# New slots for every piece beside the scan in a fused token, scan and FFN kernel

## The chip, the cores and the metric

The kernel runs on one core of one Trainium2 chip. The metric is the device time of the core in microseconds (us); lower is better. Five engines work side by side, each through its own list of instructions in order: TensorE (PE), VectorE (DVE), ScalarE (ACT), GpSimd (POOL) and SyncE (SP), which here only issues DMAs. They meet by semaphores.

## The reference

32 images of 224 x 224 and 32 texts of 77 tokens of 256 go in. Cut to what matters:

```python
# 1 tokens: 14 x 14 patches of 16 x 16 x 3, layer norm (768), matmul to 256, layer norm
p = patches(x); y = layernorm(layernorm(p, g1, b1) @ W + bias, g2, b2)
h = concat([y, txt], axis=1)                     # 196 + 77 = 273 positions
# 2 scan, on every second position of layernorm(h)
xs = rmsnorm(layernorm(h)[:, ::2]) * g_norm
x_proj, gate = split(xs @ w_in.T + b_in)
for t in positions:                              # state: 32 x 256 x 64
    s = tanh(s * A + x_proj[t][:, :, None] * Bm)
    y[t] = s @ c_sum + Dv * x_proj[t]
h = h + repeat((y * silu(gate)) @ w_out.T + b_out, 2)
# 3 FFN on layernorm(h), int weights / 127, hidden 768
h = h + (silu(z @ w_gate.T) * (z @ w_up.T)) @ w_down.T
```

The scan is the part that can't be done out of order: each position needs the state of the one before.

## The kernel before, in words

Positions are taken in 20 groups of 14 (one row of patches of all 32 images, or 14 text tokens; the last group has 7). A group has 7 scan steps, since every second position is scanned. The work of a group is spread over several iterations of a software pipeline. In iteration i, group i+1's raw pixels are read and normalised (`ahead`), group i is turned, embedded and projected (`pre`), group i-1 is scanned (`scan`), group i-2 goes from the scan's output through attention's output, residual, normalisation and FFN up to the hidden product (`post`), and group i-3 is multiplied by the down weights and stored (`down`).

One iteration has 56 slots: 7 steps of 8 chunks. In each slot the scan does one *grow* on DVE (line 827, U = h * A, into one of four PSUM banks), one *drive* on PE (line 1380, adds x * B to the bank) and one *squash* on ACT (line 1093, h = tanh(U)). A grow waits for the squash of four slots before, which frees its bank. All other work is cut into pieces, and the dictionary `PLANS` gives for each piece the slot behind whose scan instruction it stands on its engine. There is one plan for each kind of iteration: "zero" (i = -1) and "first" (i = 0), which have no scan, so that slots are only an order; "second" (i = 1); "image" (12 iterations, i = 2 to 13); "text" (6 iterations); "last" (i = 20, four steps of scan) and "tail" (no scan). Within a slot the pieces stand in the order of the calls in the body. The slots of different engines aren't bound to each other: an engine runs on until a semaphore stops it.

Pieces that the text speaks of: `turn` (PE) and `xT_copy` (ACT) transpose normalised pixels, `embed` (PE) multiplies them by W, `average` (PE) and raw_means, raw_deviation, raw_variance, raw_shift (DVE) make the pixels' statistics, `normalise` (ACT and GpSimd) applies them. `tok_stats`, `tok_shift`, `ln_stats`, `ln_shift` (DVE) with `token_rsqrt`, `ln_rsqrt`, `token_tiles` (GpSimd) normalise tokens. `turn_xa`, `xaT_copy`, `project`, `x_copy`, `x_low_part` make the scan's input, which SP writes to memory and loads back spread out as x_diag: early steps at the end of the same iteration, late steps in the next. `gate_silu` and `skip_term` make the gate.

The scan's output is read out once a step by `read_step` (line 1390: 8 matmuls of fp32 into the bank Y, 16 records in the trace). It needs the eight squashes of its step. Its place is fixed: in slot 3 of the following step, and the last step's readout in slot 3 of the next iteration. `y_copy` (ACT, line 1099) takes Y out; SP writes it to y_scr and loads it back as yT (lines 707, 713), GpSimd's `gating` (1267, 1272) adds the skip term and multiplies by the gate, `attend` (PE) multiplies by w_out, and `residual` (DVE, line 959) adds the tokens, which SP loads (`res`, line 750) behind the stores of the output (743). Then res_stats, res_variance, res_shift, fx_apply, turn_fx, fxT_copy, fx_low_part; then six blocks of FFN: ffn_gate and ffn_up (PE), ffn_silu (ACT), ffn_product (DVE), act_high_part (ACT), act_low_part (GpSimd). In the next iteration `shrink` (PE) multiplies by the down weights once all six low parts are there, and `finish` (DVE, line 995) adds the result to res.

SP's order is written out in `sync_body` and isn't changed: raw loads, gate_in, y_scr writes, yT loads, out stores, res load, late x_diag, tok store, scan writes, early x_diag, gate store. GpSimd has an order of its own, `POOL_ORDER`.

Of the kernel before, what the change touches and what calls it, by code (L numbers as in the profile page):

```python
# [34 lines left out]
READ_AT = 3  # L35
# [20 lines left out]
def span(first, end):  # L56
# [11 lines left out]
        shrink=(1, 2, 3, 5, 7, 7, 7, 7), turn=(8, 8, 9, 13, 13, 13, 13, 14), attend=(16, 16), average=(17, 21),  # L68
        embed=(17, 17, 17, 20, 21, 23, 23, 24, 25, 25, 28, 28), turn_fx=(30, 30), ffn_gate=(34, 38, 39, 42, 46, 50),
        ffn_up=(34, 38, 42, 44, 50, 52), turn_xa=(37,), project=(39, 39, 46, 48), finish=(8, 11), raw_patch=(10, 10,  # L70
        11, 11, 11, 12, 12, 12, 12, 14, 14, 14, 16, 16), raw_means=(17,), raw_deviation=(21,), raw_variance=(23,),
        res_stats=(20,), res_variance=(22,), res_shift=(27,), fx_low_part=(34, 34), tok_stats=(26, 32),
        tok_shift=(27, 34), ln_stats=(35,), ln_shift=(37,), raw_shift=(27,), x_low_part=(43,), ffn_product=(37, 41,
        43, 46, 53, 55), y_copy=(2,), xT_copy=(8, 8, 9, 12, 12, 12, 12, 15), fx_apply=(26, 27, 28, 28),
        fxT_copy=(30, 30), tok_normalise=(26, 34), ln_apply=(34,), xaT_copy=(36,), x_copy=(39,), gate_silu=(48,),
        ffn_silu=(33, 37, 39, 43, 46, 50), act_high_part=(37, 40, 40, 46, 50, 53), normalise=(38, 39, 49, 49, 51,
        52, 53), residual=(19,)),
    "text": dict(
        shrink=(5, 5, 7, 8, 12, 13, 16, 16), attend=(22, 25), turn_fx=(34, 34), ffn_gate=(35, 39, 41, 45, 49, 50),
        ffn_up=(37, 40, 44, 47, 49, 52), turn_xa=(27,), project=(30, 30, 32, 32), finish=(15, 20), res_stats=(30,),  # L80
        res_variance=(30,), res_shift=(31,), fx_low_part=(36, 36), ln_stats=(23,), ln_shift=(27,), x_low_part=(43,),
        ffn_product=(40, 44, 47, 50, 54, 55), y_copy=(2,), fx_apply=(31, 31, 31, 31), fxT_copy=(32, 32),
        ln_apply=(26,), xaT_copy=(27,), x_copy=(30,), gate_silu=(31,), ffn_silu=(35, 38, 43, 46, 46, 49),
        act_high_part=(44, 51, 51, 54, 55, 55), residual=(30,)),
    "last": dict(
        shrink=(5, 6, 7, 7, 9, 13, 13, 17), attend=(22, 25), turn_fx=(37, 37), ffn_gate=(40, 46, 50, 54, 55, 55),
        ffn_up=(45, 46, 50, 54, 55, 55), finish=(15, 19), res_stats=(30,), res_variance=(32,), res_shift=(32,),
        fx_low_part=(36, 43), ffn_product=(50, 50, 50, 51, 55, 55), y_copy=(2,), fx_apply=(32, 32, 34, 39),
        fxT_copy=(39, 43), ffn_silu=(44, 47, 47, 53, 55, 55), act_high_part=(48, 49, 54, 55, 55, 55),
        residual=(30,), y_next=(55,)),  # L90
    "first": dict(
        turn=(1, 1, 1, 1, 1, 1, 7, 9), embed=(1, 4, 4, 10, 10, 12, 13, 16, 19, 23, 31, 34), weight_turn=(1, 1, 1,
        1), weight_copy=(1, 8, 16, 55), xT_copy=(0, 0, 0, 0), first_copy=(0, 1, 4, 13), tok_stats=(18, 45),
        tok_centre=(20, 35), tok_affine=(28, 36), tok_shift=(46,), tok_normalise=(16,), ln_stats=(40,),
# [92 lines left out]
def build(nc, x, txt, W, tok_bias, ln1_g, ln1_b, ln2_g, ln2_b, w_in, b_in, A, Bm, Cm, Dv, w_out, b_out,  # L187
# [8 lines left out]
    with ctx:  # L196
# [1546 lines left out]
```

## Time and profile before

| | us |
|---|---|
| median of the runs shown (3) | 1350.34 |
| lowest and highest | 1347.21, 1351.81 |
| profiled execution: span | 1347.8 |
| PE busy | 1203.9 (89%) |
| DVE busy | 1066.3 (79%) |
| ACT busy | 982.1 (73%) |
| POOL busy | 423.5 (31%) |

The span is the time from the first to the last instruction of one execution; the profile reports no time around it. An engine's busy time is the union of its instructions' times, from start to end; instructions that follow each other overlap at their ends, so a piece's spacing is shorter than its duration. A scan iteration is counted from its first grow to the next one's.

### The profile page before, as it was taken

To read this page: it belongs to the slowest core of one execution; us is meant where nothing else is said; L and a number is where in the kernel's file an instruction comes from. 1 tells how busy PE (TensorE), PEld (TensorE's weight loads), DVE (VectorE), ACT (ScalarE), POOL (GpSimd) and SP (SyncE) were. 2 spreads that over 40 slices of the span, in tenths; PEclk is the share of its full clock that TensorE was granted. 3 is DMA by queue.
4 is the path that set the end of the run, shared out by engine and by line. 5 is a ranking of instruction groups with operands and counts; after the bars stand their busy time and mean duration, and the time that the engine had idled before them with its cause. 6 is when DMAs were issued, how large, how long until landed. Compare 5 with 4: busy or idle time off the path is not lost.

```text
span 1347.8 us, 26044 instructions
## 1 busy us (share of the span) xinstructions
PE 1203.9 (89%) x7217; PEld 642.2 (48%) x7217; DVE 1066.3 (79%) x2423; ACT 982.1 (73%) x1944; POOL 423.5 (31%) x435
## 2 busy tenths in 40 slices
PE   6678898999999999999999999999999899998977
PEld 4434445454545464646464646464444444444435
DVE  4697888887878887888888878777888888887843
ACT  2357596969696969696969696968778788787752
POOL 6413152525252525252525252514121221321220
PEclk9779899999999999999999999999999999999989
DMA  7411414141414141414141414212322322322210
GB/s 173 130 28 36 102 49 103 49 102 49 101 49 101 49 101 49 101 49 101 49 101 49 101 49 101 62 47 63 82 72 66 104 56 79 93 65 61 63 43 27
DMA packets 154814, 99.60 MB, mean 74 GB/s; under 512 B 129072, under 2 KB 143536, under 8 KB 153424
## 3 DMA queue, kind: packets, MB, share of 16 engines
q1 hardware_dynamic: 151120, 97.58, 28.4%
q10 hardware_dynamic: 3648, 1.46, 0.5%
q8 instruction: 23, 0.38, 0.1%
q14 instruction: 23, 0.19, 0.0%
HBM read 58.39 MB, written 40.60 MB: 73 GB/s over the span
## 4 chain that ended last, share of the span: by engine, by line
PE 31%; issue 26%; POOL 18%; DVE 8%; ACT 7%; DMA 7%; SPq 2%; POOLq 1%; ACTq 0%; DVEq 0%
PE Y L1390 8%; PE U L1380 6%; POOL xT_act L1309 4%; DVE U L827 4%; DMA y_scr<-y_fx 4%; PE P L1560 3%; PE P L1561 3%; POOL rawn L1288 3%; PE P L1576 2%; ACT h L1093 2%; POOL raw_s L1256 2%; PE P L1577 2%; DMA yT<-y_scr 2%; POOL tok L1301 2%; POOL tok L1304 2%
## 5 line engine op out<-in xcount | busy, mean ns | idle before, releaser
L827 DVE TENSOR_TENSOR U<-h,a_col 128x512 f32<-128x512 f32 x1096 | 708.9, 690 | 145.6 <-ACT h L1093 138.9
L1093 ACT ACTIVATE h<-U 128x512 f32<-128x512 f32 x1096 | 609.2, 608 | 200.4 <-PE U L1380 198.5
L1380 PE MATMUL U<-x_diag,b_st 128*128 128x512 f16 x1096 | 363.1, 386 | 51.4 <-DVE U L827 49.8
L1390 PE MATMUL Y<-h,read_st 128*32 128x512 f32 x2192 | 268.7, 608 | 0.7 <-ACT h L1093 0.7
L1380 PEld LDWEIGHTS U<-x_diag,b_st 128*128 128x128 f16 x1096 | 104.1, 99 | 250.6 <-DVE U L827 198.4
L1309 POOL TENSOR_TENSOR xT_act<-act,xT_act 128x448 f16<-128x448 f32 x114 | 117.4, 1038 | 242.5 <-ACT xT_act L1202 242.5
L1456 PE MATMUL P<-tok_w,xT_act 128*112 128x256 f32 x648 | 158.7, 385 | 0.8 <-ACT xT_act L1117 0.8
L1456 PEld LDWEIGHTS P<-tok_w,xT_act 128*112 128x112 f32 x648 | 116.9, 181 | 31.5 <-ACT xT_act L1117 1.1
L1390 PEld LDWEIGHTS Y<-h,read_st 128*32 128x32 f32 x2192 | 57.8, 110 | 133.7 <-issue 117.0
L1576 PE MATMUL P<-down_w,xT_act 128*112 128x256 bf16 (+1 forms) x480 | 114.8, 277 | 5.9 <-POOL xT_act L1309 4.2
L1577 PE MATMUL P<-down_w,xT_act 128*112 128x256 bf16 (+1 forms) x480 | 113.7, 275 | 0.0
L1267 POOL TENSOR_TENSOR yT<-yT,gate_in 128x448 f32<-128x448 f32 x20 | 22.7, 1136 | 244.9 <-DMA yT<-y_scr 244.9
L1560 PE MATMUL P<-fx_split,gate_w 128*128 128x448 f16 x228 | 81.0, 355 | 12.0 <-DVE fx_split L990 10.6
L984 DVE SCALAR_TENSOR_TENSOR act<-fsg,P 128x448 f32<-128x448 f32 (+1 forms) x118 | 72.1, 611 | 21.2 <-PE P L1561 18.1
L1117 ACT ACTIVATE xT_act<-P 128x384 f32<-128x384 f32 x108 | 80.4, 795 | 8.4 <-PE P L1439 7.0
L1560 PE MATMUL P<-fx_split,up_w 128*128 128x448 f16 (+1 forms) x236 | 83.0, 353 | 0.7 <-DVE act L984 0.7
L1561 PE MATMUL P<-fx_split,up_w 128*128 128x448 f16 (+1 forms) x236 | 82.9, 352 | 0.0
L1197 ACT ACTIVATE fsg<-P 128x448 f32<-128x448 f32 x114 | 63.6, 558 | 24.4 <-PE P L1561 22.9
L1561 PE MATMUL P<-fx_split,gate_w 128*128 128x448 f16 x228 | 80.8, 354 | 0.0
L1256 POOL TENSOR_TENSOR res_s<-res_s,half_th 112x4 f32<-112x4 f32 x20 | 20.6, 1028 | 186.2 <-DVE res_s L973 186.2
L834 DVE BATCH_NORM_STATS2 raw_st<-raw 96x6 f32<-96x256 f32 x196 | 70.1, 409 | 10.0 <-DMA raw<-in_x 9.7
L1491 PE MATMUL P<-xaT,in_w 128*128 128x224 f32 x320 | 74.3, 370 | 1.7 <-ACT xf L1165 1.0
(165 smaller groups left out, 1469.1 us busy)
## 6 DMA issues: line engine op xcount, KB each, us to landing
raw<-in_x SPq DMA_DIRECT2D x42, 448.0 KB, 6.1
gate_scr<-gate_o SPq DMA_DIRECT2D x20, 448.0 KB, 2.5
gate_in<-gate_scr SPq DMA_DIRECT2D x20, 448.0 KB, 7.6
tok_scr<-tok SPq DMA_DIRECT2D x19, 448.0 KB, 3.1
res<-tok_scr SPq DMA_DIRECT2D x19, 448.0 KB, 3.7
out<-res SPq DMA_DIRECT2D x76, 112.0 KB, 2.3
x_diag<-scan_scr SPq DMA_DIRECT2D x312, 16.0 KB
x_diag<-scan_scr SPq DMA_DIRECT2D x304, 12.0 KB
```

The lines of the kernel that those rows point to most:

```text
L827: dve.tensor_tensor(U[bank_of(slot)][:, :].rearrange("p (l b) -> p l b", b=B), h[:, (slot - CHUNKS) % RING, :].rearrange("p (l b) -> p l b ...
L1093: sc.activation(h[:, slot % RING, :], U[bank_of(slot)][:, :], ACT.Tanh, scale=1.0 / U_SCALE).then_inc(squashed, 1)
L1117: sc.activation(xT[:, hf * CH:hf * CH + CH, par, :].rearrange("p c (b t) -> p t c b", t=STEPS)[:, t0:t0 + nt], P[turn_bank(n)][:, 0:nt * R ...
L1309: gp.tensor_tensor(act_lo[:, k, :], act[:, k, :], act_hi[:, k, :], ALU.subtract).then_inc(act_lo_done, 1)
L1380: pe.matmul(U[bank_of(slot)][:, :], b_st[:, c, :], x_diag[:, c, :, t * B:t * B + B], start=False, stop=True, skip_group_check=True).then_i ...
L1390: mm = pe.matmul(Y[c4 * 32:c4 * 32 + 32, :], read_st[:, t, half, :], h[:, (t * CHUNKS + half * RG + c4) % RING, :], start=(t == 0 and half ...
L1456: mm = pe.matmul(tok_bank(k // 2, g)[0:PT, (k % 2) * D:(k % 2) * D + D], xT[:, f, k // 2, (k % 2) * PT:(k % 2) * PT + PT], tok_w[:, f, :], ...
L1491: mm = pe.matmul(P[1][:, k * TOK:k * TOK + TOK], in_w[:, j, e0:e0 + 128], xaT[:, j, :], start=(j == 0), stop=(j == DB - 1))
L1560: pe.matmul(bank, half, fx_hi[:, j, 0:n], start=(j == 0), stop=False)
L1561: mm = pe.matmul(bank, half, fx_lo[:, j, 0:n], start=False, stop=(j == DB - 1))
L1576: pe.matmul(bank, act_hi[:, f, k * m:k * m + m], half, start=(f == 0), stop=False)
L1577: mm = pe.matmul(bank, act_lo[:, f, k * m:k * m + m], half, start=False, stop=(f == HB - 1))
```

## The change

Every list of slots in `PLANS` is new, and so is GpSimd's order. `read_step` becomes a piece with its own list, `read`: entry 0 is the readout of the last step of the iteration before, entry k that of step k-1. Two waits are added: raw_shift waits, in image iterations, until all eight turns of its group are done, and the FFN's first block waits for its inputs in the up half as well as in the gate half.

```diff
-READ_AT = 3
     "image": dict(
-        shrink=(1, 2, 3, 5, 7, 7, 7, 7), turn=(8, 8, 9, 13, 13, 13, 13, 14), attend=(16, 16), average=(17, 21),
-        embed=(17, 17, 17, 20, 21, 23, 23, 24, 25, 25, 28, 28), turn_fx=(30, 30), ffn_gate=(34, 38, 39, 42, 46, 50),
-        ffn_up=(34, 38, 42, 44, 50, 52), turn_xa=(37,), project=(39, 39, 46, 48), finish=(8, 11), ...
-        ... y_copy=(2,), xT_copy=(8, 8, 9, 12, 12, 12, 12, 15), fx_apply=(26, 27, 28, 28), ...
-        ... normalise=(38, 39, 49, 49, 51, 52, 53), residual=(19,)),
+        read=(0, 12, 18, 29, 33, 42, 51), shrink=(2, 2, 4, 5, 6, 6, 8, 8), turn=(8, 9, 10, 10, 11, 12, 13, 16),
+        attend=(16, 16), average=(18, 20), embed=(18, 19, 19, 20, 21, 22, 24, 24, 26, 27, 28, 28), turn_fx=(31,
+        32), ffn_gate=(35, 36, 39, 40, 47, 53), ffn_up=(35, 39, 42, 46, 51, 53), turn_xa=(38,), project=(40, 41,
+        47, 48), finish=(8, 11), ... y_copy=(0,),
+        xT_copy=(8, 8, 8, 10, 10, 12, 12, 17), fx_apply=(22, 24, 25, 29), ...
+        ... normalise=(28, 28, 28, 29, 42, 47, 49), residual=(19,)),
     "text": dict(
-        shrink=(5, 5, 7, 8, 12, 13, 16, 16), attend=(22, 25), turn_fx=(34, 34), ffn_gate=(35, 39, 41, 45, 49, 50),
-        ffn_up=(37, 40, 44, 47, 49, 52), ... finish=(15, 20), ... y_copy=(2,), ... residual=(30,)),
+        read=(0, 13, 21, 29, 36, 41, 53), shrink=(3, 4, 6, 8, 10, 15, 19, 20), attend=(23, 24), turn_fx=(39,
+        39), ffn_gate=(43, 45, 46, 48, 50, 51), ffn_up=(44, 45, 46, 48, 50, 51), ...
+        finish=(13, 22), ... y_copy=(0,), ... residual=(32,)),
     "last": ...
-        ... y_copy=(2,), ... residual=(30,), y_next=(55,)),
+        read=(1, 11, 19, 28), ... y_copy=(1,), ... residual=(40,), y_next=(40,)),
     "first": ...
-        ... weight_copy=(1, 8, 16, 55), ... raw_patch=(20, 20, 24, 24, ...), tok_stats=(18, 45), project=(44, 46, 46, 46),
-        clear_banks=(55,), clear_stage=(52,), ...
+        ... weight_copy=(7, 11, 17, 33), ... raw_patch=(11, 11, 16, 16, ...), tok_stats=(15, 42), project=(25, 39, 42, 50),
+        clear_banks=(43,), clear_stage=(11,), ...
     "second": ...
-        ffn_turn=(41, 43, 44, 47, 48, 51, 55, 55, 55, 55, 55), ... ffn_cast=(1, 2, 3, 7, 8), ffn_max=(5, 9, 23, 26, 31, 35),
+        read=(4, 8, 21, 27, 36, 44, 50), ffn_turn=(31, 36, 39, 40, 41, 45, 48, 49, 51, 53, 55), ...
+        ffn_cast=(0, 0, 0, 0, 0), ffn_max=(2, 4, 4, 5, 6, 21), ...
     # "tail", "zero" and POOL_ORDER: the same pieces in other places; clear_rest comes first in "first",
     # ln_rsqrt before token_rsqrt(1) in "image"
...
             def raw_shift():
                 dve.wait_ge(raw_rstd, r + 1)
+                if pre and image:
+                    dve.wait_ge(turned_ps, (g + 1) * 8)
...
             def ffn(k, which):
-                if k == 0 and which == 0:
+                if k == 0:
                     pe.wait_ge(fxT_done, (q + 1) * 4)
                     pe.wait_ge(fx_lo_done, (q + 1) * 2)
...
                     drive(slot)
-                    if slot % CHUNKS == READ_AT and slot >= CHUNKS:
-                        read_step(slot // CHUNKS - 1, s, steps)
-                    elif slot == READ_AT and due(s):
-                        read_step(STEPS - 1, s - 1, STEPS)
+                    for k in parts_at(plan, "read", slot):
+                        if k:
+                            read_step(k - 1, s, steps)
+                        elif due(s):
+                            read_step(STEPS - 1, s - 1, STEPS)
```

## Rows read from the trace of the kernel before

**Rows 1.** The page: busy time of an engine, and the chain that ended last.
```profile
PE 1203.9 (89%) x7217; PEld 642.2 (48%) x7217; DVE 1066.3 (79%) x2423; ACT 982.1 (73%) x1944; POOL 423.5 (31%) x435
...
PE 31%; issue 26%; POOL 18%; DVE 8%; ACT 7%; DMA 7%; SPq 2%; POOLq 1%; ACTq 0%; DVEq 0%
```
**Rows 2.** Windows: stretch, length, busy PE, PEld, DVE, ACT, POOL, clock, DMA share, GB/s.
```profile
0.00:62.60 62.60, 39.81 (x176) 26.66 (x177) 34.21 (x125) 16.75 (x30) 35.80 (x30) 0.89 0.56 143
62.60:135.20 72.60, 57.50 (x294) 28.61 (x292) 59.97 (x142) 46.01 (x88) 15.23 (x18) 0.88 0.20 48
...
672.80:740.20 67.40, 62.14 (x382) 34.46 (x381) 55.49 (x135) 52.44 (x105) 24.64 (x26) 1.00 0.30 75
1047.90:1100.90 53.00, 48.93 (x302) 23.35 (x301) 45.44 (x86) 42.84 (x86) 11.81 (x13) 1.00 0.29 80
```
**Rows 3.** Groups by line of the image iteration from 672.8: busy, mean ns, idle before.
```profile
L827 DVE TENSOR_TENSOR U<-h,a_col 128x512 f32<-128x512 f32 x56 | 36.5, 689 | 7.6 <-ACT h L1093 7.5
L1093 ACT ACTIVATE h<-U 128x512 f32<-128x512 f32 x57 | 32.2, 611 | 10.8 <-PE U L1380 10.8
...
L1456 PE MATMUL P<-tok_w,xT_act 128*112 128x256 f32 x48 | 11.5, 379 | 0.0
```
**Rows 4.** Waits of the same iteration: total, times, longest.
```profile
POOL yT L1267 <- DMA yT<-y_scr: 14.3, 1, 14.3
...
DVE U L827 <- ACT h L1093: 7.5, 12, 2.2
```
**Rows 5.** Timeline of PE in that iteration: start, length, instruction, idle before.
```profile
671.84 0.35 PE L1561 MATMUL P<-fx_split,up_w 128*128 128x448 f16 x1
...
674.82 0.32 PE L1576 MATMUL P<-down_w,xT_act 128*112 128x256 bf16 x1 [0.32 <-POOL xT_act L1309]
...
676.75 1.92 PE L1390 MATMUL Y<-h,read_st 128*32 128x512 f32 x16
678.60 0.32 PE L1576 MATMUL P<-down_w,xT_act 128*112 128x256 bf16 x1
...
694.37 0.38 PE L1380 MATMUL U<-x_diag,b_st 128*128 128x512 f16 x1
...
739.30 0.35 PE L1561 MATMUL P<-fx_split,up_w 128*128 128x448 f16 x1
```
**Rows 6.** Chain of waits in that iteration: start, length, what.
```profile
678.82 0.61 ACT y_fx L1099
...
681.03 4.60 DMA y_scr<-y_fx
...
686.35 2.52 DMA yT<-y_scr
```
**Rows 7.** Timelines of SP (DMA issues) and DVE in that iteration.
```profile
674.46 1.36 SPq L371 DMA_DIRECT2D raw<-in_x  x3
...
692.52 0.35 SPq L750 DMA_DIRECT2D res<-tok_scr  x1
...
696.48 1.23 DVE L959 SCALAR_TENSOR_TENSOR res<-P,res 112x1024 f32<-112x1024 f32 x1 [0.88 <-DMA res<-tok_scr]
```
**Rows 8.** Timeline of DVE in the text iteration from 1047.9.
```profile
1071.95 1.23 DVE L959 SCALAR_TENSOR_TENSOR res<-P,res 112x1024 f32<-112x1024 f32 x1
```
**Rows 9.** Timeline of the start: staging area cleared, x_lo, first drive.
```profile
52.52 2.30 DVE L457 MEMSET x_diag<- 128x2688 int32 x1 [0.74 <-issue]
...
54.74 0.56 DVE L949 SCALAR_TENSOR_TENSOR x_lo<-xf,x_hi 128x448 f16<-128x448 f32 x1
...
64.11 0.38 PE L1380 MATMUL U<-x_diag,b_st 128*128 128x512 f16 x1
```
**Rows 10.** Lines of FFN casts and maxima: duration ns min/median/max, first and last start.
```profile
L552 DVE CAST act<-act x2: 675/814/954, 63.8 to 65.5; 128x1536 f32<-128x1536 int32 x1, 128x1024 f32<-128x1024 int32 x1
...
L557 DVE TENSOR_REDUCE large<-act x2: 1214/1483/1752, 68.7 to 76.2; 128x1 f32<-128x1536 f32 x1, 128x1 f32<-128x1024 f32 x1
```
**Rows 11.** Timeline of GpSimd in the last iteration with FFN.
```profile
1315.51 1.13 POOL L1267 TENSOR_TENSOR yT<-yT,gate_in 128x448 f32<-128x448 f32 x1 [2.21 <-DMA yT<-y_scr]
```

More of the change, by code:

```diff
@@ L73 @@
[L73 to L77, printed above, removed]
-    "text": dict(
-        shrink=(5, 5, 7, 8, 12, 13, 16, 16), attend=(22, 25), turn_fx=(34, 34), ffn_gate=(35, 39, 41, 45, 49, 50),
[L80 to L84, printed above, removed]
@@ L85 @@
-    "last": dict(
[L86 to L90, printed above, removed]
-    "first": dict(
-        turn=(1, 1, 1, 1, 1, 1, 7, 9), embed=(1, 4, 4, 10, 10, 12, 13, 16, 19, 23, 31, 34), weight_turn=(1, 1, 1,
-        1), weight_copy=(1, 8, 16, 55), xT_copy=(0, 0, 0, 0), first_copy=(0, 1, 4, 13), tok_stats=(18, 45),
-        tok_centre=(20, 35), tok_affine=(28, 36), tok_shift=(46,), tok_normalise=(16,), ln_stats=(40,),
-        ln_shift=(44,), ln_apply=(3,), ln_apply_first=(47,), turn_xa=(42,), xaT_copy=(23,), project=(44, 46, 46,
-        46), x_copy=(25,), x_low_part=(54,), gate_silu=(55,), raw_patch=(20, 20, 24, 24, 26, 34, 34, 34, 36, 36, 38,
-        42, 44, 46), raw_means=(48,), average=(37, 43), raw_deviation=(50,), raw_variance=(51,), raw_shift=(51,),
-        normalise=(33, 36, 39, 39, 39, 43, 49), clear_banks=(55,), sum_c=(36,), read_scale=(55,), b_split=(5, 9, 9,
-        14, 18, 39), c_pair=(3,), clear_stage=(52,), diag_half=(51,), keep_busy=(52, 54, 55)),
@@ new lines @@
+    "last": dict(
+        read=(1, 11, 19, 28), shrink=(0, 3, 5, 7, 8, 15, 15, 16), attend=(22, 26), turn_fx=(34, 37),
+        ffn_gate=(38, 43, 49, 51, 52, 54), ffn_up=(41, 45, 49, 51, 53, 54), finish=(15, 19), res_stats=(41,),
+        res_variance=(43,), res_shift=(43,), fx_low_part=(44, 44), ffn_product=(45, 50, 50, 53, 53, 55),
+        y_copy=(1,), fx_apply=(32, 32, 33, 36), fxT_copy=(36, 37), ffn_silu=(37, 38, 44, 45, 49, 55),
+        act_high_part=(38, 44, 47, 54, 55, 55), residual=(40,), y_next=(40,)),
@@ new lines @@
+    "tail": dict(
+        shrink=(3, 4, 6, 9, 11, 18, 19, 21), attend=(11, 16), turn_fx=(24, 24), ffn_gate=(28, 32, 40, 46, 49,
+        55), ffn_up=(34, 39, 48, 51, 54, 55), finish=(0, 5), res_stats=(0,), res_variance=(0,), res_shift=(7,),
+        fx_low_part=(22, 28), ffn_product=(28, 29, 32, 47, 50, 52), fx_apply=(0, 6, 12, 13), fxT_copy=(29, 41),
+        ffn_silu=(42, 42, 47, 47, 53, 55), act_high_part=(43, 51, 51, 55, 55, 55), residual=(0,),
+        act_low_tail=(39, 44, 50, 52, 53, 55), keep_busy=(2, 20, 21, 26)),
@@ L119 @@
+        average=(8, 9), bias_part=(14, 22, 31, 35, 49, 54), normalise=(3, 13, 28, 30, 31), bias_add=(45,),
         keep_busy=(0, 0, 4)),
```

86 lines of the change are left out of this document (50 added, 36 removed).

## The prediction, made before the change was run

> **What bounds the kernel now.** I read the page first, then the stages by windows, then one steady image iteration by lines, waits, timeline and chain, then the start. The page has TensorE busy for 89% of the span, but the chain that ends last is 31% PE, 26% issue, 18% POOL, 8% DVE [rows 1]: no engine is the bound alone; the time is set by how four in-order queues are laid against each other. By windows a steady image iteration takes 67.4 us, with PE busy 62.1, DVE 55.5 and ACT 52.4; a text iteration 53.0 with 48.9, 45.4 and 42.8; the second iteration 72.6 with 57.5 and 60.0 [rows 2]. PE's busy time has the tails of its pipelined matmuls in it. Worked out by spacing instead (start to start where pieces follow each other), an image iteration has 56 drives of 0.22, seven readouts of 1.85 (676.75 to 678.60), 8 shrink pieces near 0.7, 12 embed pieces of 0.9 (the row gives at most 11.5/12) and some 17 us of turns, attend, FFN and projection: about 58 us. So some 9 us of 67.4 are PE waiting, which is the most that an order could give back [rows 2, 3, 5]. The waits between grow and squash are spread out: DVE waits 7.5 us for ACT in 12 pieces, and the longest single wait is GpSimd's, 14.3 us for yT to land [rows 4].
>
> **The image iteration, 12 of them, piece by piece.** The number of instructions is the same; only places change, plus two waits. I walked the new lists against the old ones in three stretches, each engine's pieces in order with the spacings above, and 0.1 us for each hand-over.
>
> *Head.* The last up piece is followed by three drives and then nothing until the first shrink piece at 674.82, 2.8 us later, because the shrink needs product, high part and GpSimd's low part of the last FFN block; five drives fill 1.1 of it, so PE loses 1.7 [rows 5]. The new list puts the previous step's last readout (1.85) at slot 0, in that hole. It can't start before squash 55, which I place 1.6 us after the last up piece: 1.1 us of waiting is left in place of 1.7, and the readout no longer stands between the shrink pieces. I put squashes 0 and 1 around y_copy: ACT waits for the readout at slot 0 instead of slot 2, 2 us in both. So the shrinks (slots 2 to 8) end at 1.7 + 1.85 for the readout + 8 x 0.69 + 8 drives of 0.22 = 10.8 us after the last up piece; before it was 11.5. From there to attend's end PE has a readout of 1.85, eight drives (1.8), eight turns (2.3) and attend (2.0), 8.0 us. Before it took 10.8, as turns waited for finish(1) and for xT copies; with the copies grouped (ACT slots 8, 10, 12) and the readout between the turns I leave 1.2 of waiting. Attend's end goes from 22.3 us (694.37) to 20.0 [rows 5].
>
> *The readout's own chain.* y_copy at 678.82 starts a chain of transfers: 4.60 us of y_scr, 2.52 of yT, then GpSimd's gating [rows 5, 6]. SP issues in order, so the out stores and the load of res stand behind it: res is issued at 692.52, and residual (696.48) still waited 0.88 us for it [rows 7]. The new y_copy comes 3.1 us earlier after the last up piece. Gating then ends before attend wants it, and the next lock on res is finish(1), whose store must have landed: finish(1) is 0.4 to 0.9 us earlier, and SP's queue 3. Residual's end goes from 25.6 us to between 22.7 (SP alone) and 24.1 (one wait of 1.2 at average kept). I take 24.1, being the nearer to the row.
>
> One rule speaks against this. Raw's three transfers are issued at 674.46 and gate_in's behind them, ahead of y_scr, and y_scr took 4.60 us to land [rows 6, 7]. The Trainium skill, "DMA: Bandwidth & Descriptors", section "Two DMAs through the same engine are not ordered", has descriptors of one queue start in order: an earlier y_scr would then only wait longer behind raw. By that rule the head start is lost unless raw moves too; it does (ACT's last normalise goes from slot 53 to 49), and I expect the head start to survive. Without it the sum would be rival 1's, worked out below.
>
> *From residual to the last up piece.* Before: from residual's end (696.48 + 1.14 of spacing = 697.62) to the end of the last up piece (739.30 + 0.19 = 739.49) it is 41.9 us; both ends by spacing, as the piece before ends at 672.03 [rows 5, 7]. New: PE does one readout before residual and two embed pieces more behind it, equal work. fx_apply(0) at slot 22 makes ACT wait for res_shift (DVE slot 25) with squashes 23 to 25 behind it, about 1.5 us, which PE's embed pieces cover; readout 4 at slot 33 and 5 at 42 wait 0.3 us for the squash; up 3 waits 0.8 us for product 2. With the same work as before my walk gives 41.6, so I claim almost nothing here. Together 24.1 + 41.6 = 65.7 against 67.4: -1.7 us each, -20 us for 12. Bounds: no gain, if the head start is absorbed at average; and -2.8.
>
> **Text, 6 iterations of 53.** FFN moves from slots 35 to 52 into 43 to 51, y_copy from 2 to 0, turn_fx to 39. Residual stood 24 us into the iteration (1071.95) [rows 8]; finish(1) at slot 22 puts it at about 28, and the 22.6 us behind it have to hold what took 27. I get 51.7 us: -1.2 each, rounded to -6 in all because this stretch has no slack left on PE; bounds +1 and -2 each.
>
> **Start.** The first drive is at 64.11 us [rows 9]. Ahead of it stand the clearing of the staging area by DVE (2.30 us from 52.52, just before x_lo at 54.74), weight_copy 3 and clear_banks behind ACT's DMA issues. The new list clears at slot 11, projects at 25 and 39 and has weight_copy 3 at 33. The price: DVE's raw_patch 0 to 3 now stand before tok_stats(0), and raw lands only near 34 us (estimated from the start's transfers), 1.8 us later than tok_stats ran. Net, x_hi and x_lo come 3 us earlier, the early x_diag lands near 60.3 and the first drive at 60.4: -3.7. Bounds 0 and -6.
>
> **Second iteration.** Casts of the FFN weights (median 0.81 for act) and the first maximum (1.75) sat on DVE in slots 1 to 8, in the path of grows [rows 10]. At slot 0 they, with bias_split 0 to 2, run while DVE would wait for the first drive; about 6 us of DVE's 60.0 [rows 2] leave the loop. ffn_turn, five of eleven at slot 55 before, starts at 31. Against it: readout 1 at slot 8 waits about 1 us for squash 7, and average(0) waits for 14 patches. I take -5.3; bounds +2 and -8.
>
> **Last and tail.** y_next moves ahead of most silus, so gating is bound by act_low 5 instead of yT, which it waited 2.21 us for [rows 11]: -2, bounds 0 and -3. GpSimd's new order costs nothing where it waits anyway [rows 4]; its act_low 5, the piece that PE waits for, stays last.
>
> **The two new waits.** turned_ps before raw_shift was met 10 slots before. The FFN wait on a second piece repeats one met a piece earlier. No wait here has an own row; 0 to 0.05 us for each of about 50, below 2.5 us. I take 0.
>
> **Sum.** -20 - 6 - 3.7 - 5.3 - 2 = -37. The profiled execution spans 1347.8 us with nothing reported around it, 2.5 below the median 1350.3 of the runs shown: 1347.8 - 37 = 1310.8, plus 2.5 is 1313.3.
>
> **Rivals.**
> 1. *The head start is absorbed.* y_scr still lands behind raw and gate_in, residual stays at 25.6 us. For: 4.60 us of landing beside raw. Against: residual's own wait of 0.88 us. Image gains 0.4 each: -5 - 6 - 3.7 - 5.3 - 2 = -22, 1328.
> 2. *Readouts block PE; slower.* A readout directly behind its step (slots 0, 33, 42 of image; 0, 29 and 41 of text) holds drive, squash and grow behind it, where the old place, three slots on, was free. It needs squash done, and ACT runs up to 2 us behind PE. Where that wait isn't covered, 0.9 us for each of three in 18 iterations is +49; with the forecast's -37 that is +12, so 1362. It decides from 37/54, about 0.7 us a readout; my walk has 0.3 for two of the three. For it: grows already wait for ACT in 12 places [rows 4]. Against: at slot 0 PE has nothing else to do.
> 3. *No change.* The loops refill as PE's own work binds behind residual (image 0, text +1), and only start and second count, partly: -3, 1347.
> 4. *Both locks open:* image -2.8, rest as above but start -6: 1297.
>
> **Chances.** Forecast 0.44, rival 1 0.20, rival 2 0.14, rival 3 0.10, rival 4 0.12. 0.3%, about 4 us, is what a measurement of this kernel can tell from no change. Faster 0.77, same 0.09, slower 0.14. The range 1293 to 1353 leaves out rival 2 and the far end of rival 4; the forecast's own range is 1303 to 1323.
>
> **What would show it.** Right: image iterations of 65 to 66 us; y_copy 5 us or less after the last up piece, residual 24 us after it; first drive near 60; second iteration under 68; PE's idle time at the first shrink under 1 us. Wrong: waits of PE for ACT h L1093 before Y over 1 us each; DVE waiting for res at an unchanged place; an image iteration at 67 or more; text over 53.

## The result, and the profile after

The kernel after takes 1288.61 us (median of 4 runs, 1286.47 to 1290.56), the kernel before 1351.07 beside it: a ratio of 0.9547, 95% interval 0.9528 to 0.9565, or 62.5 us less. The forecast was 1313.3, 37 less, with 1293 as the low end of its range: the sign was right, the size was short by 25 us, and the time lies 4 us below the range. The profiled execution took 1288.4 us and spans 1286.7.

The page of the kernel after, the lines that answer to [rows 1]:

```profile
PE 1193.1 (93%) x7217; PEld 643.8 (50%) x7217; DVE 1078.1 (84%) x2423; ACT 982.7 (76%) x1944; POOL 434.3 (34%) x435
...
PE 46%; DVE 16%; issue 14%; ACT 11%; DMA 5%; POOL 3%; SPq 2%; DVEq 1%; ACTq 0%; POOLq 0%
```

The work is the same (7217 matmuls, 2423 and 1944 instructions). What went is waiting: the chain was 31% PE and 18% POOL, it is now 46% PE and 3% POOL, so the order of the queues is closer to being bound by TensorE's own work. ACT's busy time didn't move; DVE's rose by 12 us, and that is a cost found below (x_lo).

Windows of the kernel after, with the columns of [rows 2]: the start, the second iteration, a steady image iteration and a steady text iteration. They are cut 0.4 us ahead of the first grows, which start at 54.97, 123.16, 640.56 and 997.85; the lengths are the same.

```profile
0.00:54.60 54.60, 37.00 (x155) 26.32 (x156) 32.71 (x124) 12.91 (x22) 29.31 (x21) 0.84 0.59 151
54.60:122.80 68.20, 58.58 (x316) 29.57 (x314) 63.72 (x141) 48.24 (x95) 25.08 (x27) 0.90 0.25 61
...
640.20:704.40 64.20, 61.66 (x383) 34.59 (x381) 56.35 (x135) 53.00 (x105) 25.31 (x26) 1.00 0.32 79
997.50:1049.10 51.60, 48.98 (x309) 23.24 (x305) 45.40 (x85) 42.08 (x87) 11.79 (x13) 1.00 0.30 80
```

PE's busy time in the image iteration is the same within 0.5 us (62.1 before); 67.4 us have become 64.2. Stretch by stretch, each from the first grow to the next iteration's first grow, beside what the prediction gave it:

| stretch | before | after | difference | forecast |
|---|---|---|---|---|
| start and second iteration | 135.2 | 123.2 | -12.0 | -9.0 |
| image, 12 iterations | 805.5 | 773.0 | -32.5 | -20 |
| text, 6 iterations | 322.4 | 309.1 | -13.3 | -6 |
| last and tail | 84.7 | 81.3 | -3.3 | -2 |
| sum | 1347.8 | 1286.7 | -61.1 | -37 |

Every term came out larger, and the image term has half of the whole miss. The walk through one image iteration can be read off the timelines of the kernel after, first DVE and SP (start, length, instruction, idle before):

```profile
644.53 1.87 SPq L709 DMA_DIRECT2D y_scr<-y_fx  x4
651.10 1.27 SPq L715 DMA_DIRECT2D yT<-y_scr  x2
652.77 3.23 SPq L745 DMA_DIRECT2D out<-res  x4
657.92 0.35 SPq L752 DMA_DIRECT2D res<-tok_scr  x1
...
661.71 1.22 DVE L963 SCALAR_TENSOR_TENSOR res<-P,res 112x1024 f32<-112x1024 f32 x1 [0.30 <-DMA res<-tok_scr]
```

and PE:

```profile
639.63 0.35 PE L1565 MATMUL P<-fx_split,up_w 128*128 128x448 f16 x1
639.82 0.59 PE L1384 MATMUL U<-x_diag,b_st 128*128 128x512 f16 x2
641.31 0.39 PE L1384 MATMUL U<-x_diag,b_st 128*128 128x512 f16 x1 [0.89 <-DVE U L829]
641.63 1.92 PE L1394 MATMUL Y<-h,read_st 128*32 128x512 f32 x16
...
660.16 0.59 PE L1384 MATMUL U<-x_diag,b_st 128*128 128x512 f16 x2
...
703.82 0.35 PE L1565 MATMUL P<-fx_split,up_w 128*128 128x448 f16 x1
704.01 0.38 PE L1384 MATMUL U<-x_diag,b_st 128*128 128x512 f16 x1
```

The last up piece ends at 639.82 by spacing. The readout stands in the hole behind it, and attend ends at 660.16, 20.3 us later (forecast 20.0, before 22.3). Residual waits 0.30 us for the load of res and ends at 661.71 + 1.14 = 662.85, that is 23.0 us, where the prediction had 24.1 and its lower bound 22.7. From there to the next last up piece (704.01) it is 41.2, forecast 41.6. The waits of that iteration, with the columns of [rows 4]:

```profile
POOL yT L1271 <- DMA yT<-y_scr: 11.6, 1, 11.6
...
ACT h L1097 <- PE U L1384: 8.1, 12, 1.8
...
DVE U L829 <- ACT h L1097: 4.1, 7, 1.2
```

DVE waited 7.5 us for ACT before, now 4.1; ACT waited 10.8 for PE, now 8.1 [rows 3, 4]. The engines of the scan wait less for each other.

### The profile page after: what moved, and what is told of

Same layout as the page of the kernel before. It is cut to its first block, busy times and chain, and to the rows that moved or that the text cites. A ratio compares the mean times of both kernels' runs of the same rounds, so it can differ in the third digit from the quotient of the medians.

```text
span 1286.7 us, 26087 instructions
## 1 busy us (share of the span) xinstructions
PE 1193.1 (93%) x7217; PEld 643.8 (50%) x7217; DVE 1078.1 (84%) x2423; ACT 982.7 (76%) x1944; POOL 434.3 (34%) x435
## 4 chain that ended last, share of the span: by engine, by line
PE 46%; DVE 16%; issue 14%; ACT 11%; DMA 5%; POOL 3%; SPq 2%; DVEq 1%; ACTq 0%; POOLq 0%
PE Y L1394 11%; PE U L1384 9%; DVE U L829 7%; PE P L1460 7%; ACT h L1097 5%; PE P L1564 5%; PE P L1565 4%; DMA raw<-in_x 3%; PE P L1580 2%; PE P L1581 2%; PE P L1443 2%; PE P L1495 2%; DMA y_scr<-y_fx 1%; PE P L1515 1%; ACT fsg L1201 1%
## 5 line engine op out<-in xcount | busy, mean ns | idle before, releaser
L1384 PE MATMUL U<-x_diag,b_st 128*128 128x512 f16 x1096 | 368.7, 383 | 42.6 <-DVE U L829 40.1
L1384 PEld LDWEIGHTS U<-x_diag,b_st 128*128 128x128 f16 x1096 | 101.3, 98 | 210.9 <-DVE U L829 153.5
L1460 PEld LDWEIGHTS P<-tok_w,xT_act 128*112 128x112 f32 x648 | 113.1, 177 | 41.4 <-ACT xT_act L1121 10.1
L1564 PE MATMUL P<-fx_split,gate_w 128*128 128x448 f16 x228 | 81.3, 356 | 3.0 <-DVE fx_split L994 1.9
L836 DVE BATCH_NORM_STATS2 raw_st<-raw 96x6 f32<-96x256 f32 x196 | 71.8, 410 | 9.9 <-DMA raw<-in_x 9.7
L1495 PE MATMUL P<-xaT,in_w 128*128 128x224 f32 x320 | 77.5, 369 | 1.3 <-ACT xf L1169 0.8
L1201 ACT ACTIVATE fsg<-P 128x448 f32<-128x448 f32 x114 | 63.4, 556 | 14.5 <-PE P L1565 13.2
```

What stands on the lines that cost most here:

```text
L1384: pe.matmul(U[bank_of(slot)][:, :], b_st[:, c, :], x_diag[:, c, :, t * B:t * B + B], start=False, stop=True, skip_group_check=True).then_i ...
L1460: mm = pe.matmul(tok_bank(k // 2, g)[0:PT, (k % 2) * D:(k % 2) * D + D], xT[:, f, k // 2, (k % 2) * PT:(k % 2) * PT + PT], tok_w[:, f, :], ...
L1495: mm = pe.matmul(P[1][:, k * TOK:k * TOK + TOK], in_w[:, j, e0:e0 + 128], xaT[:, j, :], start=(j == 0), stop=(j == DB - 1))
L1564: pe.matmul(bank, half, fx_hi[:, j, 0:n], start=(j == 0), stop=False)
```

## Experiments

All runs are beside runs of the kernel before on the same chip (1349.3 to 1349.7 us). Each kernel is the kernel after with one edit unless it is said otherwise. A result is given as its median, the ratio to the kernel before with its 95% interval, and how much more it is than the kernel after (1288.61, runs from 1286.47 to 1290.56, interval 0.9528 to 0.9565). Of u_end, d_res, u_cast and n_text the interval overlaps that of the kernel after: their differences of 0.2 to 3.4 us rest on the stretches of the traces more than on the times. The length of an iteration is that of most of them in the run's trace, from first grow to first grow.

### Which part brought how much

**u_image**: the image plan and GpSimd's image order as before, with readouts at their old places.

```diff
 PLANS["image"], POOL_ORDER["image"] = those of the kernel before
+read=(3, 11, 19, 27, 35, 43, 51), y_copy=(2,)
```

> The changed kernel with the plan and GpSimd's order of the image iterations as before (readouts at slots 3, 11, ..., 51); all else changed. Theory A, each kind of iteration gained by itself, as the two traces' stretches say (image 32.5 us of 61.5): 1288.6 + 32 = 1321 us, image iterations back at 67. Rival B, the gain of a stretch hangs on its neighbours' new plans (a head that is filled because the iteration before ends otherwise): clearly off 1321, under 1310 or over 1332. By the forecast on record (20 us for images) it would be 1309.

1323.27 us, ratio 0.9799 (0.9776 to 0.9822): 34.7 more than the kernel after, as theory A has it, and its steady image iteration takes 67.0 us. Its twelve take 805.4 us, where the kernel before has 805.5: the two added waits, which stand in this kernel, cost nothing there. **u_text** does the same to text:

> The changed kernel with the plan of the text iterations as before; all else changed. Theory A: text's share in the traces is 13.3 us, of which the four steady iterations hold 5.3 and the first and the last 8.0: 1302 us. Rival B: the first text iteration's 4.3 us were the image plan's doing, so only about 9 come back: 1298 us. By the forecast (6 us): 1295.

1306.48, 0.9682 (0.9653 to 0.971): 17.9 more, beyond theory A's 13. The four steady iterations are back at 52.9, the first one gives back 2.8 us, the sixth 3.6, and the first step of the last iteration, whose plan is not touched, 4.3. **u_start** does it to the plans zero, first and second:

> The changed kernel with the plans zero, first and second as before; all else changed. Theory A: 1288.6 + 12.4 = 1301 us, first drive at 64.1 us, second iteration 72.6 us. By the forecast (9 us): 1297.6. Rival: the second iteration's end loses what it ran ahead anyway at the first image iteration, and less than 6 us come back: under 1295.

1304.11, 0.9666 (0.9644 to 0.9689): 15.5 more, with four runs from 1299.15 to 1306.46; the profiled one is the lowest, and its stretch to the end of the second iteration is 11.5 longer. **u_end** does it to last and tail:

> The changed kernel with the plans last and tail as before; all else changed. Theory A: 1288.6 + 3.3 = 1292 us, gating of the last group bound by yT again (a wait near 2.2 us). Rival: last and tail are bound by the same chain either way, and the 3.3 us came from the text plan's earlier end: under 1290.

1291.76, 0.957 (0.955 to 0.9591): 3.2 more, as theory A has it, though gating waits 1.1 us for yT in place of the 2.2 named there. The four add up to 71.3 against 62.5: between the kinds of iteration the change is nearly additive. Within one kind it is not, as the next runs show.

### The head, and the rule on the queue

**u_head** takes back only the head of image and text: `read[0]` to slot 3, `y_copy` to 2.

> The changed kernel, only the last step's readout back from slot 0 to slot 3 and y_copy from 0 to 2 in image and text. Theory A, the head start of the readout's chain is what frees the image iteration: residual moves back by 2 to 3 us, image iterations by 2 or more, text by 0 to 1: 1288.6 + 24 to 36, about 1318 us. Rival B, the hole is filled but the rest of the new list makes the gain: +0.6 an iteration, about 1300 us. Rival C, the new head costs ACT as much as it gives: within 4 us of 1288.6.

1303.22, 0.9665 (0.9649 to 0.9681): 14.6 more, of which the image iterations have 10.3, at 65.38 each. Nearest to rival B. Residual, 667.42 in the timeline of DVE below, ends 23.8 us after the last up piece (644.74) in place of 23.0, and no longer waits for res:

```profile
667.42 1.18 DVE L968 SCALAR_TENSOR_TENSOR res<-P,res 112x1024 f32<-112x1024 f32 x1
```

So the readout's move is worth 1.2 of the 3 us in this place. **b_head** makes the same move alone in the kernel before: `read[0]` and `y_copy` to slot 0.

> The kernel before (all its plans, old GpSimd order), with one thing new: the last step's readout at slot 0 and y_copy at 0 in image and text. Theory A, the chain behind y_copy bounds the image iteration: 2 us for each of 12, 0.5 for text: about 1351 - 27 = 1324 us. Rival B, the old list can't use an earlier residual, and only the hole is filled: 0.6 us in 18 iterations, 1340 us. Rival C, nothing or slower, as ACT's wait at y_copy now stands before squash 1: 1350 or more.

1364.88, 1.0117 (1.01 to 1.0134): slower than before by 15.5 us, which is rival C; 10.8 of it is in the image iterations and 1.6 in text, and 3.6 stands ahead of the first image iteration, where the plans are those of before. It is the kernel after's code with the plans of before, so the two added waits are in it. Windows of two image iterations of this kernel, with identical instructions:

```profile
477.20:545.60 68.40, 63.37 (x383) 34.85 (x381) 55.64 (x135) 52.72 (x105) 24.69 (x26) 0.98 0.30 74
682.60:749.80 67.20, 61.89 (x383) 34.56 (x381) 55.62 (x135) 52.67 (x105) 24.64 (x26) 1.00 0.30 75
```

The second takes what an iteration took before. The first has its readout 0 at a lower clock, in PE's timeline:

```profile
478.20 0.39 PE L1403 MATMUL U<-x_diag,b_st 128*128 128x512 f16 x1 [0.68 <-DVE U L848]
479.84 3.32 PE L1413 MATMUL Y<-h,read_st 128*32 128x512 f32 x16 [1.25 <-ACT h L1116]
```

16 records took 3.32 us where they take 1.92; the granted clock from 479.7 to 483.0 was 0.58, most of it at the lower level of 1.2 GHz. Ahead of it PE had waited 0.68 us for DVE and 1.25 for ACT, since in the old order ACT is later: squash 0 starts 2.2 us after the first grow, in the kernel after 1.2. Of the ten image iterations from 273.33 on, all with the wait of 1.2 us for ACT, eight have a readout 0 of 2.8 to 3.6 us and two one of 1.92. So the head move gains nothing by itself, and loses 1.2 us where the clock falls; text loses 0.5 an iteration at a granted clock of 1.00. It pays only with ACT ahead, as it is in the new order; which of ACT's pieces does that no run separates. That is the mechanism of the prediction's second rival in another form: the readout in its new place must find its squash done.

**e_rawlate** tests the rule on the queue: SP issues raw's three loads behind y_scr's writes instead of ahead.

```diff
-    load_raw(sp, r)        # at the head of SP's iteration
     y_scr writes
+    load_raw(sp, r)
```

> The changed kernel with SP's raw load issued behind the y_scr writes instead of ahead of them. Nothing is left out. Queue theory (y_scr lands behind raw and gate_in): y_scr lands 2 us or more sooner than the 6.4 us from first issue to last landing that it takes now, gating starts that much earlier; raw lands later, near 11 us into the iteration, behind raw_patch's slots, so DVE waits for it and the time rises by 0 to 2 us an iteration: 1289 to 1312. Rival (transfers share bandwidth, order doesn't matter): y_scr still takes 6 us or more.

1383.74, 1.0253 (1.0223 to 1.0283): 95 more, far outside the 1289 to 1312 that were expected. The chain of its iteration from 709.13, and SP's, DVE's and GpSimd's timelines in it:

```profile
712.27 0.61 ACT y_fx L1105
...
716.41 7.78 DMA raw<-in_x
```
```profile
713.09 1.85 SPq L705 DMA_DIRECT2D y_scr<-y_fx  x4
715.37 1.36 SPq L375 DMA_DIRECT2D raw<-in_x  x3
716.92 1.29 SPq L717 DMA_DIRECT2D yT<-y_scr  x2
...
724.22 0.42 DVE L838 BATCH_NORM_STATS2 raw_st<-raw 96x6 f32<-96x256 f32 x1 [6.83 <-DMA raw<-in_x]
...
725.04 1.13 POOL L1273 TENSOR_TENSOR yT<-yT,gate_in 128x448 f32<-128x448 f32 x1 [13.56 <-DMA yT<-y_scr]
```

yT is issued 7.8 us into the iteration, as soon as raw's issues are through, where the kernel after issues it at 10.5; so y_scr does land earlier when raw isn't ahead of it. By the packets in the two traces its last one ends 3.7 us after y_copy starts, instead of 6.6. In the kernel after y_scr is issued at 644.53, but its packets start at 648.43, when the last of raw's has ended at 648.07; here they start 0.8 us after the issue. But yT now stands behind raw and takes 7.2 us to land (median of the run) instead of 2.6, and gating starts 15.9 us into the iteration against 13.9. The queue serves what came first; moving raw only chooses who waits. DVE waits 6.83 us for raw, PE stands still meanwhile, and the granted clock of the iteration is 0.93 where it was 1.00. Eleven of the twelve image iterations take 72.4 to 74.0 us; how much of the 8 to 10 us more is the wait and how much the clock no run separates. By the rule of the Trainium skill that the prediction weighed ("DMA: Bandwidth & Descriptors", section "Two DMAs through the same engine are not ordered") descriptors of one queue start in order: the trace agrees, with 2.6 us against 7.2 for the same transfer. In the kernel after raw is issued 0.5 us ahead of the iteration's first grow (640.04), where it was 1.7 us into it [rows 7]. So y_scr still lands behind raw, only all of it earlier: its last packet ends 9.7 us into the iteration, before 12.1. Of the 2.9 us that y_copy gained on the last up piece 2.4 survived, as the prediction expected.

### Inside the image iteration

**u_front** puts back the pieces of the front: shrink, turn, xT_copy, average, embed, finish, raw's statistics and res_stats.

> Kernel after, but in image iterations the front pieces stand at the old slots: shrink, turn, xT_copy, average, embed, finish, raw_patch, raw_means, raw_deviation, raw_variance, res_stats, res_variance. Readouts, y_copy, residual, fx_apply, FFN and all behind keep their new slots, GpSimd its new order. Theory A (the image gain of 3 us sits ahead of residual: the new order of these pieces lets turns, attend and average run without waits): an image iteration 66.2 or more, 12 x 2 = +24: about 1313. Theory B (with the readout at slot 0 kept, the rest of the front is worth little): at most +0.5 each, under 1295. Theory C (mixed lists collide): over 1325.

1306.07, 0.9677 (0.9653 to 0.9701): 17.5 more, an image iteration of 65.92. Nearest to theory A in size, but not in place: residual ends at 672.22 + 1.13 = 673.35, 23.45 us after the last up piece (649.90), 0.4 later than in the kernel after; the other 1.3 us come behind residual. The old places of embed and of the statistics reach behind it; which of them costs that isn't separated. **u_back** puts back the FFN and the projection behind residual.

> Kernel after, but in image iterations the back pieces stand at the old slots: FFN gate, up, silu, product, high parts, turn_fx, fxT_copy, fx_low_part, turn_xa, xaT_copy, project, x_copy, x_low_part. The rest is the kernel after, readouts 33, 42 and 51 included. Theory A (what stands behind residual brought 0.4 to 0.7 us an iteration, as the stretch from residual to the last FFN block shrank from 41.9 to 41.2 us): +0.7 each, about 1297. Theory B (order behind residual is worth nothing): 1289. Theory C (the old FFN places don't go with the new readouts, which stand at other slots between them): over 1305.

1340.79, 0.9937 (0.9918 to 0.9956): 52 more, 68.62 for an image iteration, longer than the 67.4 of the kernel before, at a granted clock of 1.00. Theory C. ACT's timeline of that kernel shows the place:

```profile
724.75 0.56 ACT L1221 ACTIVATE xT_act<-act 128x448 f16<-128x448 f32 x1
727.67 0.58 ACT L1221 ACTIVATE xT_act<-act 128x448 f16<-128x448 f32 x1 [2.36 <-DVE act L1003]
728.15 1.06 ACT L1112 ACTIVATE h<-U 128x512 f32<-128x512 f32 x2
```

Two high parts stand at slot 40. The second waits for a product whose FFN block is now behind the readout at slot 42, where before it was ahead of the readout at 43; it waits 2.36 us (0.39 in the kernel before) and the squashes behind it with it, and with them grow. That is a part of the 4.4 us; the rest isn't traced. **u_reads** is the mirror of it: all readouts of image and text back at their old slots, the rest new.

> The changed kernel with all seven readouts of image and text back at slots 3, 11, 19, 27, 35, 43, 51 and y_copy at 2; all other pieces new. Theory A: like the head alone plus at most 0.5 us an iteration, about 1320 us. Rival B, readouts close behind their step (33, 42, 41) block PE, so that the old places are better for these: faster than the run with only the head undone.

1419.59, 1.0524 (1.0505 to 1.0542): 131 more than the kernel after, 71.8 us an image iteration, 57.1 to 58.8 a text iteration, and neither theory. PE's timeline:

```profile
745.33 1.20 PE L1389 MATMUL U<-x_diag,b_st 128*128 128x512 f16 x2 [1.49 <-DVE U L834]
746.46 2.85 PE L1399 MATMUL Y<-h,read_st 128*32 128x512 f32 x16
749.25 0.36 PE L1569 MATMUL P<-fx_split,gate_w 128*128 128x448 f16 x1
```

The readout at slot 35 now stands ahead of the first FFN block instead of two slots before it. PE waits 1.49 us for DVE ahead of it, and it takes 2.85 us at a granted clock of 0.65 over the stretch; the first silu waits 3.12 us for its FFN block. What else goes into the 7.6 us of an iteration isn't traced. **d_res** tests how tight the path is: `residual` at DVE's slot 21 instead of 19.

> Only residual of image iterations differs from the kernel after: at DVE's slot 21 instead of 19. By the windows of the kernel after that puts its start from 21.1 to about 24.1 us into the iteration (grow 20 and 21 run ahead of it; grow 20 would wait for squash 16 only, grow 21 for squash 17). Theory A (everything from residual to the last FFN block is one path with no slack, which is what the prediction's split of the image iteration assumes): residual's end comes 1.2 us later (two grows), an image iteration 65.4, 12 x 1.2 = +14: about 1303. Theory B (slots behind residual have slack that the pieces can use): image within 0.3 us of 64.18, at most 1292. Theory C: residual earlier isn't what limits, grow 20 first lets the scan run ahead: faster, under 1285.

1292.04, 0.957 (0.9547 to 0.9593): 3.4 more, 64.6 an iteration. Nearest to theory B. Residual ends 23.8 us after the last up piece in place of 23.0, and the iteration is only 0.42 longer: half of the delay is taken up behind it. The path from residual on isn't rigid.

### The second iteration

**u_cast**: casts, five maxima and the first bias pieces of the second iteration near their old slots.

> Only DVE's plan of the second iteration differs from the kernel after: the casts of the FFN weights at slots 1, 2, 3, 7, 8, five of the six maxima at slots 5 to 10 and the first bias pieces at 1 to 6, much as before the change, everything else of the kernel after kept. Theory A (the prediction's: these pieces, about 6 us of DVE, were moved under the wait for the first drive, and that is most of what the second iteration gained): it gets 5 us longer, about 1293. Theory B (most of the gain of some 10 us in this iteration comes from the rest: embed, turns and ffn_turn that start earlier): 1289 to 1291. Theory C (they delay raw's statistics too): over 1296.

1290.94, 0.9562 (0.9535 to 0.9588): 2.3 more, of which the iteration itself has 1.4. Theory B: what the prediction took for the cause is worth a quarter of its 5.3 us, or less: the times alone don't tell 2.3 us from nothing. A possible reason is in DVE's timeline of the kernel after:

```profile
55.57 3.26 DVE L554 CAST act<-act 128x1536 f32<-128x1536 int32 x2
```

Two casts that took 0.95 and 0.68 us take 3.26 while GpSimd works beside them. In u_cast they are back at 0.95 and 0.73, so some 1.6 us of faster casts are set against its loss. **u_fturn**: the eleven turns of the FFN weights and their copies at their old slots.

> Kernel after, but the second iteration turns the FFN weights at the old slots (five of eleven pieces at slot 55, with their copies). Theory A (these pieces stood alone at the end of the second iteration before, some 5 to 6 us in which the scan's last slots were done, and that they now lie between the slots is most of what this iteration gained): +5, about 1294. Theory B (they filled time in which the next iteration's start waited anyway): at most +1, 1290.

1299.0, 0.9626 (0.9602 to 0.9649): 10.4 more, and the second iteration takes 79.0 us in place of 68.2. Twice theory A, and longer than the 72.6 of the kernel before. The end of that iteration in PE's timeline:

```profile
128.26 0.39 PE L1389 MATMUL U<-x_diag,b_st 128*128 128x512 f16 x1 [0.55 <-DVE U L834]
...
129.92 0.44 PE L583 MATMUL P<-cst,fx_split 128*128 128x128 f32 x2 [0.69 <-ACT up_w L589]
...
132.26 0.47 PE L583 MATMUL P<-cst,y_fx 128*128 128x128 f32 x1 [0.69 <-ACT down_w L589]
...
134.16 0.47 PE L583 MATMUL P<-cst,y_fx 128*128 128x128 f32 x1 [0.79 <-DVE down_w L594]
```

The last drive is done at 128.6 and the next iteration's first grow comes at 134.0. Between them PE turns a little, waits for a copy, turns again: a chain of hand-overs between PE, ACT and DVE with nothing beside it. The kernel before has the same chain, in its timeline of all engines:

```profile
129.90 0.60 PE L576 MATMUL P<-cst,act 128*128 128x128 f32 x4
...
131.57 0.44 PE L576 MATMUL P<-cst,fx_split 128*128 128x128 f32 x2 [1.07 <-ACT up_w L582]
...
135.17 1.28 DVE L827 TENSOR_TENSOR U<-h,a_col 128x512 f32<-128x512 f32 x2
```

and the kernel after has not:

```profile
122.35 0.59 PE L1384 MATMUL U<-x_diag,b_st 128*128 128x512 f16 x2
...
123.16 0.69 DVE L829 TENSOR_TENSOR U<-h,a_col 128x512 f32<-128x512 f32 x1
```

From the last drives to the next first grow it was 5.3 us (129.90 to 135.17), in u_fturn it is 5.4, and in the kernel after 0.8 from the start of the last two drives. So the chain at the end was worth about 5 us. The other half of u_fturn's 10.8 lies ahead of it and isn't traced.

### Two tries for more

**n_pool** came from a row that we had not expected. x_lo (128 x 448, reading xf and x_hi) by its line in the kernels before, after, and in this run (duration in ns, min/median/max):

```profile
L949 DVE SCALAR_TENSOR_TENSOR x_lo<-xf,x_hi x20: 560/624/627, 54.7 to 1250.4; 128x448 f16<-128x448 f32 x20
```
```profile
L953 DVE SCALAR_TENSOR_TENSOR x_lo<-xf,x_hi x20: 616/1884/2059, 52.0 to 1188.4; 128x448 f16<-128x448 f32 x20
```
```profile
L960 DVE SCALAR_TENSOR_TENSOR x_lo<-xf,x_hi x20: 616/624/626, 51.6 to 1183.1; 128x448 f16<-128x448 f32 x20
```

In the kernel after it meets GpSimd, by the engines' timelines, and PE's next drive waits:

```profile
691.31 1.09 POOL L1292 TENSOR_SCALAR rawn<-raw,raw_s 96x256 f32<-96x256 f32 x2
...
691.99 1.89 DVE L953 SCALAR_TENSOR_TENSOR x_lo<-xf,x_hi 128x448 f16<-128x448 f32 x1 [0.65 <-ACT x_hi L1174]
...
692.37 1.03 POOL L1313 TENSOR_TENSOR xT_act<-act,xT_act 128x448 f16<-128x448 f32 x1
...
694.55 0.39 PE L1384 MATMUL U<-x_diag,b_st 128*128 128x512 f16 x1 [0.88 <-DVE U L829]
```

The edit changes GpSimd's image order alone: it has nothing to do while x_lo runs.

```diff
-("normalise", 0), ("token_tiles", 1), ("normalise", 1), ("normalise", 2), ("act_low_part", 0), ("act_low_part", 1), ...
+("normalise", 0) to ("normalise", 6), ("act_low_part", 0), ("token_tiles", 1), ("act_low_part", 1), ...
```

> Only GpSimd's order in image iterations differs from the kernel after: all normalises and the low part 0 stand ahead of token_tiles(1), so GpSimd computes nothing while DVE makes x_lo. Theory A (x_lo, 1.88 us in the middle in image iterations of the kernel after against 0.62 before, is slowed because GpSimd's xT_act low part reads SBUF beside it, and PE's drive 46 waits for it): x_lo falls back to about 0.6 us, an image iteration from 64.18 to about 63.2, 12 x -1.0 = -12: about 1277 us. Theory B (x_lo is slow from another cause, such as its place behind its reader's data, or the ACT work beside it): x_lo stays near 1.9 us, image stays at 64.2, 1288 us. Theory C (the later low parts and the later token_tiles delay shrink or the projection): above 1292.

1282.66, 0.95 (0.9477 to 0.9523): 5.9 less than the kernel after, the best of all. x_lo is at 0.624 throughout, so theory A holds for the cause. A steady iteration takes 63.4, which is 0.8 less. Half of the expected 12 us isn't there, by windows of three of its image iterations, of which two have a lower granted clock:

```profile
380.50:443.80 63.30, 61.39 (x381) 34.63 (x381) 55.47 (x135) 52.64 (x105) 25.34 (x27) 1.00 0.32 79
571.00:636.30 65.30, 62.85 (x381) 35.23 (x381) 55.42 (x135) 52.65 (x105) 25.33 (x27) 0.97 0.31 77
185.80:253.40 67.60, 63.28 (x381) 35.61 (x381) 55.65 (x135) 52.66 (x105) 25.43 (x27) 0.97 0.30 75
```

**n_text**: in text the first shrink piece ahead of readout 0 (`shrink` from slot 0, `read[0]` and `y_copy` at 1).

> Only text iterations differ from the kernel after: shrink(0) at slot 0, then readout 0 and y_copy at slot 1. In the text iterations of the kernel after PE waits for squash 55 at slot 0 while the last FFN block's parts come in. Theory A (PE can do one shrink piece in that time): -0.7 us each, 6 iterations, about 1285. Theory B (the shrink waits for GpSimd's low part 5 and holds the readout and y_copy behind it, and with them yT and attend): a text iteration 0.5 to 2 us longer, 1291 to 1300.

1288.83, 0.9549 (0.9523 to 0.9576): no difference. Steady text iterations are 0.5 us shorter (51.1), as theory A has it, but the first one takes 53.45 in place of 50.07 at a granted clock of 0.97: its shrink waits 1.25 us for GpSimd's low part and the readout behind it takes 2.86 us in place of 1.92. That is theory B's wait, in one iteration of six.

## Why the prediction was right and wrong

**Right, with the numbers:** the mechanism of the head. Readout 0 in the hole behind the last FFN block, attend 20.3 us after the last up piece (forecast 20.0), y_copy 3.9 us after it (5 or less), waits for Y small, and y_scr's head start kept (2.4 us). The two added waits cost nothing in the image iterations (u_image, 805.4 us for 805.5). The sign of every term held.

**Image, -32.5 for -20: the step "I take 24.1, being the nearer to the row" failed.** Both bounds were worked out, SP's queue at 22.7 and one kept wait at average at 24.1, and the trace gave 23.0: residual waits 0.30 us for res and for nothing else, so SP alone is the bound. The wait at average was kept because it was there before; u_front, with the old places of average, embed and the other front pieces under the new head, has residual's end at 23.45, so all of them together, that wait among them, were worth 0.4 and not 1.2. The step cost 1.1 us an iteration. The other 0.4 came behind residual (41.2 for 41.6). By the mean of 12 iterations the gain is 2.7, by the steady one shown 3.3. The image term of rival 4, "both locks open", was 2.8: it is what came true, and it had a chance of 0.12.

**"From residual to the last up piece ... I claim almost nothing here" was right as a number and wrong as a reading.** The prediction priced the new readouts at 0.3 us each over an otherwise equal walk. u_back and u_reads show that the new readouts and the new places behind residual belong together: either with the other's old places costs 4.4 and 7.6 us an iteration (1.2 of the 7.6 is the head, by u_head). With work counted as equal, the walk had no sign that the two hang on each other. The second rival (blocked readouts, +12) is nearest to them in kind; no run shows its price of 0.9 us a readout.

**Second iteration: a right sum from a wrong cause.** Start and second got -12.0 for -9.0. The first drive came at 62.15 by the trace, 2.0 us earlier for a forecast of 3.7: x_lo was 2.7 us earlier (forecast 3), but the early x_diag, placed at 60.3, came near 62, as PE waits 1.28 us for it up to the drive. From the first drive to the next iteration's first grow it was 71.1 us and is 61.0, 10 less for 5.3. **The step "about 6 us of DVE's 60.0 leave the loop" failed:** putting the casts and maxima back costs 1.4 to 2.3 us (u_cast). The turns of weights at slot 55, which it named in a clause, were worth about 5 (5.3 us from last drive to next grow before, 0.8 after): the hand-overs stand there with nothing beside them, and no wait of them was priced. That the sum of start and second was within 3 us of the measured one is luck. Where the other 3 or 4 us of this iteration come from no run shows.

**Text, -13.3 for -6.** A steady iteration takes 51.6 for 51.7, partly by luck: residual starts at 26.6 us and not at 28, and from its end on it takes 23.8 and not 22.6, so that two misses cancel. **The step that failed is "-1.2 each, -6 in all"**, which treated six iterations as alike: the first gave 4.3 and the last 3.7, where image's work runs out or the next kind begins. The rows of these two weren't read. Of the first one's 4.3 u_text gives back 2.8 and u_image 0.7. **Last and tail** gave 3.3 for 2: y_next early, and the last gating without a wait for yT, as the walk had it.

What stays open: which of ACT's pieces in the old order makes b_head's readout late; when exactly the clock falls, as two iterations with the same instructions differ in it; and why the four parts add up to 71 and not 62.5, where u_text's 4.3 us in the last iteration and the spread of 7 us in u_start's runs have a share.

## What to carry to other kernels

When every place in several in-order queues moves at once, a walk along one path gives the sign and the order of size, and a wait taken over from the old trace must be justified anew: if the piece that caused it has moved, the nearer bound isn't the old row. Look first for pieces that stand alone at the end of a stage, as a small busy time there can be a long chain of hand-overs, and read the boundary iterations, not only the steady one. And test a list as a whole: taking back a part of a good one cost from 0.4 to 7.6 us an iteration, and a move that is good in its place made the old kernel slower.

## What the runs showed of the hardware

A DVE instruction with two inputs in SBUF, the memory that both engines work from, took 1.88 to 2.06 us beside GpSimd's rawn and xT_act in place of 0.62 (x_lo, in 11 image iterations), 0.99 beside the end of one xT_act (884.35), 0.62 in every text iteration, where GpSimd did nothing beside it, and 0.62 again when only GpSimd's order was changed. Its end, 693.8, comes 0.4 us after the end of GpSimd's xT_act (693.40), which started after it. That would fit being kept out for whole instructions; no run shows it. Not every GpSimd instruction does it: at 52.02 it took 0.63 us beside raw_s (51.02 to 53.60). The Trainium skill, "SBUF — State Buffer", section "Who interferes with whom", has a DVE instruction with two SBUF inputs contend with a GpSimd one that reads SBUF; the trace agrees, with these numbers. The casts at 55.57 (3.26 us for two that took 1.63) read one input each; GpSimd's piece beside them took 1.86 for its usual 1.28. In u_cast they take 0.95 and 0.73 with GpSimd at work beside them too, so what slows them stays open.

The granted clock fell to 0.58 and 0.65 for single readouts in b_head and u_reads, behind PE waits of 1.9 and 1.5 us, and cost 1.4 and 0.9 us in the two shown. The same waits with no fall stand in two of the ten iterations of b_head, so the wait alone doesn't decide it. The stretch is short enough that the page's 40 slices barely show it (the whole run of b_head has 0.970); the windows of one iteration do.
